# Local attention of a decoder kernel: one product per head on 64 rows, softmax over eight heads at once, and another order of the slots

## The chip, the cores and the metric

The kernel runs on one core of one Trainium2 chip. A core has engines that run side by side and meet at semaphores: PE (TensorE, matrix products), DVE (VectorE), ACT (ScalarE), POOL (GpSimd) and SP (SyncE, which starts transfers). The metric is the device time of one execution in microseconds (us), the median of the runs.

## What is computed

The reference is a decoder of two blocks on 32 sequences of 128 tokens with 128 features: a bidirectional state-space layer, cross attention and a mixture of experts with two experts a token, then local attention, cross attention and a mixture with one expert a token. The part that matters here is the local attention, cut from the reference to its mathematics, for one sequence `x` (128 x 128):

```
h      = layernorm(x)
q      = rmsnorm(h @ wq.T)  as 16 heads of 64      k, v = h @ wk.T, h @ wv.T  as 4 heads of 64, k with rmsnorm
score  = q_head @ k_(head//4).T / 8, allowed where i >= j and i - j < 64
x      = x + concat_heads(softmax(score) @ v_(head//4)) @ wo.T
```

## The kernel before

`window_attention_layer` (from L1743) computes this for 32 sequences, all of whose `x` stays in SBUF. T is 128 tokens, HL 16 heads, KVL 4 key/value heads, HDL 64 features a head, QH 4 heads a "quad", NQ 4 quads a sequence, NP 8 pairs of heads.

The work is a software pipeline. `walk_sequences` calls, on every engine, `slot(b, q)` for b = sequence and q = 0 to 3; `b.plus(k)` is the sequence k later, which is skipped where it isn't real. Within a slot an engine does its pieces in the order in which they stand in the text, each for its own sequence. Each piece waits for semaphores and raises one; `due(...)` drops waits for counts that aren't positive. The last argument of `walk_sequences` says how many sequences ahead the earliest piece works: it sets how many iterations are written out ahead of and behind the hardware loop.

The steps of one sequence, with the lines of the profile:

- SP loads the two experts' outputs into `back` (L1798); POOL adds them into `both` (L2076); DVE adds that to x (L1981), takes statistics (L2021, L2023, L2025); POOL makes the reciprocal root `xr` by a power (L2082); DVE normalises into `xh` (L2018).
- PE turns `xh` (L1859), ACT evicts it to `xT` (L1932), PE projects q into `pq` and k, v into `pkv` (L1867, L1869).
- ACT squares q and k (L1950, L1953) and copies v (L1958). DVE sums the squares (L2031) and makes `mean_sq` (L2035). POOL raises it to the power -0.5 in one instruction on 20 values a token (L2099, `r`). DVE multiplies q and k with it (L2042, L2045), writing each k head twice.
- PE turns qn and kn (L1878, L1881); ACT evicts `qT` (L1938, two) and `kT` (L1943, two halves of 64 partitions). `kT` holds k twice per head: in the upper 64 rows for one head of a pair, in the lower 64 rows for the other, with zeros elsewhere, which are written once ahead of the loop (L1968).
- Per quad, `scores`: PE writes the mask into one of two PSUM tiles `ps` with an identity product (L1829) and adds two products of 128 rows and 256 columns, each for a pair of heads (L1831). DVE takes the maximum `top` (L1996) and subtracts it (L2009), ACT takes the exponential (L1919), DVE sums (`den`, L1990) and inverts (`rden`, L2003), POOL multiplies (L2089, semaphore `norm_ready`).
- `turn` (L1819) turns the four heads of a quad into `pt`; ACT evicts `prT` (L1925); `values` multiplies with v into `py` in two halves of 64 columns of the array (L1843); ACT evicts `cT` (L1913). The projection back is L1890, then DVE adds it to x (L2059) and takes statistics (L2062).

Which piece stands in which slot sets the order. Before, in slot q: PE turn(b, q), scores(b+1, q), then in slot 1 the turns of xh (b+3) and of q and k (b+2), in slot 2 the projections (b+3) and the projection back (b-1), and at the end values of the quad before. ACT: cT of two quads before, Exp, prT(b, q), then in slot 1 xT, qT and kT, in slot 2 the squares. POOL: slot 0 `both` (b+4) and a normalisation; slot 1 a normalisation; slot 2 `xr` (b+4) and a normalisation; slot 3 a normalisation and the power (b+3). DVE makes `mean_sq` (b+3) in slot 3.

Of the kernel before, what the change touches and what calls it, by code (L numbers as in the profile page):

```python
# [36 lines left out]
QH = 4  # L37
# [1705 lines left out]
def window_attention_layer(nc, S, W, routed, ahead):  # L1743
# [12 lines left out]
    with ExitStack() as ctx:  # L1756
# [17 lines left out]
        kT = [A.sb(f"kT{p}", [128, KVL, 2, T]) for p in range(2)]  # L1774
        top, den, rden = ([A.sb(f"{n}{q}", [128, QH]) for q in range(NQ)] for n in ("top", "den", "rden"))
        pr = [A.sb(f"pr{q}", [128, QH, T]) for q in range(NQ)]
        prT = [A.sb(f"prT{q}", [128, QH, T]) for q in range(2)]
        cT = [A.sb(f"cT{p}", [128, NP, T]) for p in range(2)]
        ps = [A.ps(f"ps{k}", [128, QH, T]) for k in range(2)]
# [7 lines left out]
            exp_ready den_ready rden_ready norm_ready pt_mm prT_ready y_mm cT_ready o_mm x_ready stats kT_zero""".split()}  # L1787
        routed_in = [A.sem(f"routed_in{p}") for p in range(2)]
        rows_of = routed.rearrange("(k r) d -> r k d", k=K0)
        with nc.Block() as block:  # L1790
# [16 lines left out]
            def _(pe):  # L1807
# [4 lines left out]
                def turn(b, q):  # L1812

                    t = b.quad(q)
                    pe.wait_ge(s["norm_ready"], t + 1)
                    if due(t):
                        pe.wait_ge(s["prT_ready"], t)
                    for i in range(QH):
                        ins = tr(pt[:, i, :], pr[q][:, i, :], S.ident[:, :])  # L1819
                    ins.then_inc(s["pt_mm"], 1)  # L1820

                def scores(b, q):
                    t = b.quad(q)
                    if q == 0:
                        pe.wait_ge(s["qT_ready"], 2 * (b.n + 1))
                        pe.wait_ge(s["kT_ready"], 2 * (b.n + 1))
                    if due(t - 1):
                        pe.wait_ge(s["sub_ready"], t - 1)
                    mm(ps[q % 2][:, :, :], S.ident_bf[:, :], bc(outside[:, :], 1, QH), start=True, stop=False)  # L1829
                    for k in range(2):  # L1830
                        ins = mm(ps[q % 2][:, 2 * k:2 * k + 2, :], qT[b.p][:, 2 * q + k, :], kT[b.p][:, q, :, :],  # L1831
                                 start=False, stop=k == 1)
                    ins.then_inc(s["s_mm"], 1)

                def values(b, q):
# [6 lines left out]
                    for k in range(2):  # L1842
                        ins = mm(py[64 * k:64 * k + 64, 0:2 * T], v[b.p][:, q, :], prT[q % 2][:, k:QH:2, :],  # L1843
                                 start=True, stop=True)
                    ins.then_inc(s["y_mm"], 1)

                def slot(b, q):
                    if b.real():
                        turn(b, q)
                    nxt = b.plus(1)  # L1850
                    if nxt.real():
                        scores(nxt, q)
                    n = b.plus(3)
                    o = b.plus(-1)
# [5 lines left out]
                    if q == 2 and n.real():  # L1860
                        pe.wait_ge(s["xT_ready"], n.n + 1)
                        if due(2 * n.n):
                            pe.wait_ge(s["qT_ready"], 2 * n.n)
                        if due(2 * n.n):
                            pe.wait_ge(s["kT_ready"], 2 * n.n)
                        for k in range(2):
                            mm(pq[k][:, :], xT[:, :], W.wq[:, 512 * k:512 * k + 512], start=True, stop=True  # L1867
                               ).then_inc(s["qkv_mm"], 1)
                        mm(pkv[:, :], xT[:, :], W.wkv[:, :], start=True, stop=True).then_inc(s["qkv_mm"], 1)  # L1869
                    m = b.plus(2)  # L1870
                    if q == 1 and m.real():
                        pe.wait_ge(s["qn_ready"], 2 * (m.n + 1))
                        pe.wait_ge(s["kn_ready"], m.n + 1)
                        pe.wait_ge(s["ve_ready"], m.n + 1)
                        for k in range(2):
                            for i in range(4):
                                pair = 4 * k + i
                                ins = tr(pq[k][:, i * T:(i + 1) * T], qn[:, 2 * pair:2 * pair + 2, :], S.ident[:, :])  # L1878
                            ins.then_inc(s["qkT_mm"], 1)
                        for i in range(KVL):  # L1880
                            ins = tr(pkv[:, i * T:(i + 1) * T], kn[:, i, :, :], S.ident[:, :])  # L1881
                        ins.then_inc(s["qkT_mm"], 1)
                    if q == 2 and o.real():
# [8 lines left out]
                    last = b if q else b.plus(-1)  # L1892
                    if last.real():
                        values(last, (q - 1) % NQ)

                walk_sequences(pe, slot, 4)

            @block.scalar
            def _(act):
                A_ = nc.scalar.activation  # L1900
                act.wait_ge(s["kscale"], 2)
                act.wait_ge(s["kT_zero"], 2)

                def slot(b, q):

                    y = b if q >= 2 else b.plus(-1)
                    if y.real():
# [8 lines left out]
                    if e.real():  # L1916
                        qe = (q + 2) % NQ
                        act.wait_ge(s["sub_ready"], e.quad(qe) + 1)
                        A_(pr[qe][:, :, :], pr[qe][:, :, :], ACT.Exp).then_inc(s["exp_ready"], 1)  # L1919
# [6 lines left out]
                    n = b.plus(3)  # L1926
                    m = b.plus(2)
# [5 lines left out]
                    if q == 1 and m.real():  # L1933
                        if due(NQ * (m.n - 1)):
                            act.wait_ge(s["s_mm"], NQ * (m.n - 1))
# [5 lines left out]
                        for k in range(2):  # L1941
# [3 lines left out]
                    if q == 2 and n.real():  # L1945
# [9 lines left out]
                    if q == 3 and n.real():  # L1955
# [5 lines left out]
                walk_sequences(act, slot, 4)  # L1961

            @block.vector
            def _(dve):
                V = nc.vector
                dve.wait_ge(W.loaded, W.all())
                for p in range(2):
                    V.memset(kT[p][:, :, :, :], 0.0).then_inc(s["kT_zero"], 1)  # L1968
# [6 lines left out]
                def slot(b, q):  # L1975
                    d = b if q < 3 else b.plus(1)
                    w = b.plus(4)
                    if q == 1 and w.real():
                        i = bass.ds(w.n, 1)
                        dve.wait_ge(s["both_ready"], w.n + 1)  # L1980
                        V.tensor_tensor(S.x[:, i, :], S.x[:, i, :], both[w.p][:, :, :], ALU.add  # L1981
                                        ).then_inc(s["in_ready"], 1)
                        dve.wait_ge(s["in_ready"], w.n + 1)
                    if q == 2 and w.real():
                        dve.wait_ge(s["xbn_ready"], w.n + 1)
                    if d.real():
                        qd = (q + 1) % NQ
                        t = d.quad(qd)
                        dve.wait_ge(s["exp_ready"], t + 1)
                        V.tensor_reduce(den[qd][:, :], pr[qd][:, :, :], AX.X, ALU.add).then_inc(s["den_ready"], 1)  # L1990
# [645 lines left out]
```

## Time and profile before

| what | value |
|---|---|
| median of 3 runs | 2474.86 us (2468.1 to 2481.22) |
| the profiled execution | 2475.35 us, its span 2473.6 us |
| PE busy over the span | 2084.3 us (84%) |
| DVE, ACT, POOL busy | 1880.5, 1434.6, 1430.9 us (76, 58, 58%) |
| local attention | about 1514 to 2045 us of the span |

The span is the time between the first and the last instruction of the profiled execution. The stage that is changed is about a fifth of it; the other stages are the same in both kernels. "Busy" is the share of time in which an engine has an instruction in work; matrix products are pipelined, so PE's share is a little generous. In the rows below, a line of a timeline gives the start, the duration, the engine and the line of the kernel, the operation, what it writes and reads, and how many are merged; in square brackets stands how long the engine stood idle ahead of it and on whom it waited. A float product is recorded as two instructions.

### The profile page before, as it was taken

The numbers are of one execution on the slowest core, as the hardware profiler recorded it, in microseconds if no ns is written. First come the engines' busy times: TensorE is split into PE (matmuls) and PEld (weight loads), VectorE is DVE, ScalarE is ACT, GpSimd is POOL, SyncE is SP. The second block draws the span as 40 slices with busy tenths as digits, with TensorE's granted clock in tenths as the row PEclk, the third lists the DMA queues.
The fourth block names the chain that finished last, engine by engine and source line by source line (L and its number), as shares of the span: only waits on it lengthen the run. The fifth ranks groups of instructions, "written<-read, shape, count | busy, mean of one in ns | idle before, by whom it ended". The sixth has DMA issues, their size and how long they took to land. (4 is left out here: it accounts for less than half of the span.)

```text
span 2473.6 us, 43829 instructions
## 1 busy us (share of the span) xinstructions
PE 2084.3 (84%) x13248; PEld 1325.8 (54%) x13248; DVE 1880.5 (76%) x3129; ACT 1434.6 (58%) x2678; POOL 1430.9 (58%) x1094
## 2 busy tenths in 40 slices
PE   3888888888888886899874884899999998998486
PEld 1333343333333333677643773566666666776476
DVE  5999999999999997577653333788888885777445
ACT  4667676666666663466542452566666664665254
POOL 4788878777878886333244453455555542332546
PEclk7999999999999999799977997899999997999588
DMA  4222222222222221200111220000000001000442
GB/s 121 74 75 71 78 74 73 73 74 69 75 70 73 75 75 47 74 11 11 31 38 53 83 82 24 9 9 8 8 8 8 6 1 57 12 12 13 139 144 72
DMA packets 104420, 130.66 MB, mean 53 GB/s; under 512 B 33668, under 2 KB 65718, under 8 KB 103632
## 3 DMA queue, kind: packets, MB, share of 16 engines
q1 hardware_dynamic: 95600, 111.19, 15.4%
q0 software_dynamic: 8192, 17.59, 2.0%
q8 instruction: 48, 0.79, 0.1%
q10 hardware_dynamic: 512, 0.53, 0.1%
q14 instruction: 68, 0.56, 0.1%
HBM read 111.16 MB, written 25.20 MB: 55 GB/s over the span
## 5 line engine op out<-in xcount | busy, mean ns | idle before, releaser
L829 POOL TENSOR_TENSOR m_hc<-m_h,m_cs 128x1024 f32<-128x1024 f32 x256 | 602.8, 2359 | 183.2 <-DVE m_h L739 167.6
L739 DVE TENSOR_TENSOR_SCAN m_h<-m_da,m_pdb 128x1024 f32<-128x1024 f32 x256 | 585.2, 2286 | 27.7 <-DVE m_pdb L711 3.9
L432 PE MATMUL m_py<-m_hc,ident 128*128 128x512 f32 x1024 | 505.6, 618 | 1.9 <-POOL m_hc L829 1.9
L614 ACT ACTIVATE m_da<-m_dt,m_aneg 128x508 f32<-128x508 f32 x512 | 331.8, 709 | 117.2 <-DVE m_h L739 102.5
L711 DVE TENSOR_TENSOR m_pdb<-m_du,m_pdb 128x1024 f32<-128x1024 f32 x256 | 309.1, 1208 | 26.2 <-PE m_pdb L419 17.0
L432 PEld LDWEIGHTS m_py<-m_hc,ident 128*128 128x128 f32 x1024 | 199.4, 197 | 222.5 <-issue 211.8
L1082 ACT ACTIVATE x_prT<-x_pt 77x512 f32<-77x512 f32 x256 | 138.1, 586 | 135.5 <-PE x_pt L984 134.8
L1198 POOL TENSOR_TENSOR x_kd<-x_kT,x_hm 128x308 f32<-128x308 f32 x64 | 45.1, 705 | 278.7 <-ACT x_v_raw L1094 278.7
L419 PE MATMUL m_pdb<-m_bcrow,m_sel 96*128 96x512 bf16 x256 | 101.0, 396 | 111.1 <-DVE m_h L739 111.0
L2089 POOL TENSOR_TENSOR d_pr<-d_pr,d_rden 128x512 f32<-128x512 f32 x128 | 132.3, 1037 | 92.7 <-DVE d_rden L2003 92.5
L2099 POOL TENSOR_TENSOR d_r<-d_mean_sq,minus_half 128x20 f32<-128x20 f32 x32 | 113.4, 3542 | 76.1 <-DVE d_mean_sq L2035 76.1
L419 PEld LDWEIGHTS m_pdb<-m_bcrow,m_sel 96*128 96x128 bf16 x256 | 25.6, 100 | 228.0 <-DVE m_h L739 182.8
L984 PE MATMUL x_pt<-ident,x_pr 128*77 128x128 f32 x1024 | 142.0, 283 | 0.2
L984 PEld LDWEIGHTS x_pt<-ident,x_pr 128*77 128x77 f32 x1024 | 120.0, 152 | 28.3 <-issue 24.0
L1831 PE MATMUL d_ps<-d_kT,d_qT 128*128 128x256 f32 x512 | 134.1, 385 | 0.0
L378 PE MATMUL m_pm<-m_xnT,m_wtap 128*128 128x512 f32 x256 | 125.4, 614 | 1.3 <-ACT m_xnT L529 1.3
L1144 DVE TENSOR_REDUCE x_top<-x_ps 128x8 f32<-128x616 f32 x128 | 101.9, 796 | 31.3 <-PE x_ps L1003 12.4
L1728 POOL DMA_INDIRECT c_routed<-c_done,c_to x80 | 78.6, 983 | 74.6 <-DVE c_done L1699 49.7
L1150 DVE TENSOR_TENSOR x_pr<-x_ps,x_top 128x616 f32<-128x616 f32 x128 | 102.3, 800 | 15.9 <-DVE x_top L1144 3.5
L1130 DVE RECIPROCAL x_rden<-x_pyo 128x128 f32<-128x128 f32 x64 | 61.3, 958 | 68.9 <-PE x_pyo L1038 68.9
L1913 ACT ACTIVATE d_cT<-d_py 128x256 f32<-128x256 f32 x128 | 49.1, 384 | 108.6 <-PE d_py L1843 107.8
L999 PE MATMUL x_ps<-x_kd,x_qT 32*128 32x308 f32 x512 | 106.9, 495 | 4.3 <-issue 3.3
(309 smaller groups left out, 4647.8 us busy)
## 6 DMA issues: line engine op xcount, KB each, us to landing
m_cs<-crow SPq DMA_DIRECT2D x256, 256.0 KB, 3.1
f_row<-f_sorted SPq DMA_DIRECT2D x24, 400.0 KB
c_row<-c_sorted SPq DMA_DIRECT2D x40, 144.0 KB
d_back<-c_routed SPq DMA_DIRECT2D x32, 128.0 KB
f_sorted<-in_F_blank SPq DMA_DIRECT2D x9, 400.0 KB
cw_gud<-in_C_gud SPq DMA_DIRECT2D x1, 3456.0 KB
x<-in_x SPq DMA_DIRECT2D x8, 256.0 KB, 4.8
fw_w<-in_F_w SPq DMA_DIRECT2D x1, 2048.0 KB, 8.6
```

The costliest lines, as they stand in the source:

```text
L378: ins = mm(pm[1 - c][:, :], wtap[:, d, k, c * 128:(c + 1) * 128], xnT[:, par[0], :, off:off + T], start=k == 0, stop=k == TAPS - 1)
L419: mm(pdb[:, row_bank(n), :], sel[:, n, :], bcrow[d][:, :], start=True, stop=True).then_inc(s["b_mm"], 1)
L432: ins = mm(py[:, c, :], S.ident[:, :], hc[n % BUF][:, c, :], start=False, stop=n == NS - 1)
L614: A_(dst, src, ACT.Exp, scale=aneg[:, d, c, n:n + 1]).then_inc(s["da_ready"], 1)
L711: V.tensor_tensor(out, du[d][:, ::-1, :], bc(pdb[:, row_bank(n), :], 1, CH), ALU.mult).then_inc(s["db_ready"], 1)
L739: V.tensor_tensor_scan(h[n % BUF][:, way], da[n % BUF][:, d:d + CH * GT][:, way], pdb[:, b:b + 2, :].rearrange("p c t -> p (c t)")[:, way] ...
L829: P.tensor_tensor(hc[n % BUF][:, :, :], h[n % BUF][:, :].rearrange("p (c t) -> p c t", c=CH), bc(cs[n % BUF][:, :], 1, CH), ALU.mult).then ...
L984: ins = tr(pt[e][0:TC, i * T:(i + 1) * T], pr[u.p][u.h][:, QH * e + i, :], S.ident[:, :])
L1082: A_(prT[u.p][Q2 * u.h + e][:, :], pt[e][0:TC, :], ACT.Copy).then_inc(s["prT_ready"], 1)
L1831: ins = mm(ps[q % 2][:, 2 * k:2 * k + 2, :], qT[b.p][:, 2 * q + k, :], kT[b.p][:, q, :, :], start=False, stop=k == 1)
L2089: P.tensor_tensor(pr[qd][:, :, :], pr[qd][:, :, :], bc(rden[qd][:, :], 2, T), ALU.mult).then_inc(s["norm_ready"], 1)
L2099: P.tensor_tensor(r[:, :], mean_sq[:, :], S.minus_half[:, 0:NH], ALU.pow).then_inc(s["r_ready"], 1)
```

## The change

- **Scores.** `kT` is [128, KVL, T], without zeros: each k head stands in both halves of the partitions, and one eviction writes it. A head's product takes 64 rows of the array (`half`) and 128 columns; eight heads (a "pair" of quads, `pair(b, e)`, e = 0, 1) are made at once into one PSUM tile `ps` of two banks, the heads of the upper half in one bank and those of the lower in the other, ahead of them two mask products. `scores` stands in slots 0 and 2.
- **Softmax.** `top`, subtract, Exp, `den` and `rden` work on eight heads. POOL still normalises four heads at a time, two instructions in each of slots 1 and 3. `top`/subtract and `den`/`rden` stand in slots 1 and 3 of DVE, Exp in slots 0 and 2 of ACT.
- **Slots.** PE: the projections (b+3) move from slot 2 to slot 3, the turns of q and k from slot 1 to slot 2, the projection back from slot 2 to slot 1, and `values` ahead of these. ACT: qT and kT in slot 2, the squares and the copy of v in slot 3. DVE: the sum of squares and `mean_sq` in slot 0, for b+2; qn and kn in slot 2. POOL: the power in slot 0, alone; the normalisations in slots 1 and 3; `xr` and `both` (b+5) in slot 2.
- The heads are stored in another order, which `values` and the rows of `wo` follow. The walk runs five sequences ahead instead of four.

The core of the diff:

```diff
-        kT = [A.sb(f"kT{p}", [128, KVL, 2, T]) for p in range(2)]
-        top, den, rden = ([A.sb(f"{n}{q}", [128, QH]) for q in range(NQ)] for n in ("top", "den", "rden"))
-        pr = [A.sb(f"pr{q}", [128, QH, T]) for q in range(NQ)]
+        kT = [A.sb(f"kT{p}", [128, KVL, T]) for p in range(2)]
+        top, den, rden = ([A.sb(f"{n}{k}", [128, 2 * QH]) for k in range(4)] for n in ("top", "den", "rden"))
+        pr = [A.sb(f"pr{k}", [128, 2 * QH, T]) for k in range(4)]
-        ps = [A.ps(f"ps{k}", [128, QH, T]) for k in range(2)]
+        ps = A.ps("ps", [128, 2 * QH, T])
...
-                    if due(t - 1):
-                        pe.wait_ge(s["sub_ready"], t - 1)
-                    mm(ps[q % 2][:, :, :], S.ident_bf[:, :], bc(outside[:, :], 1, QH), start=True, stop=False)
-                    for k in range(2):
-                        ins = mm(ps[q % 2][:, 2 * k:2 * k + 2, :], qT[b.p][:, 2 * q + k, :], kT[b.p][:, q, :, :],
-                                 start=False, stop=k == 1)
+                    if due(pair(b, e)):
+                        pe.wait_ge(s["sub_ready"], pair(b, e))
+                    for h in range(2):
+                        mm(ps[:, of(h), :], S.ident_bf[:, :], bc(outside[:, :], 1, QH), start=True, stop=False)
+                    for i in range(QH):
+                        kv = 2 * e + i // 2
+                        for h in range(2):
+                            half = slice(64 * h, 64 * h + 64)
+                            ins = mm(ps[:, QH * h + i, :], qT[b.p][half, 2 * kv + i % 2, :], kT[b.p][half, kv, :],
+                                     start=False, stop=i == QH - 1)
                     ins.then_inc(s["s_mm"], 1)
...
+                    if nxt.real() and q % 2 == 0:
+                        scores(nxt, q // 2)
...
+                    last = b if q else o
+                    if last.real():
+                        values(last, (q - 1) % NQ)
+                    if q == 1 and o.real():
                         pe.wait_ge(s["cT_ready"], NQ * (o.n + 1))
...
+                    if q == 2 and m.real():
+                        pe.wait_ge(s["qn_ready"], 2 * (m.n + 1))
...
+                    if q == 3 and n.real():
+                        pe.wait_ge(s["xT_ready"], n.n + 1)
...
-                        for k in range(2):
-                            half = slice(64 * k, 64 * k + 64)
-                            A_(kT[m.p][half, :, k, :], pkv[half, :].rearrange("p (i t) -> p i t", t=T), ACT.Copy,
-                               scale=kscale[half, 0:1]).then_inc(s["kT_ready"], 1)
+                        A_(kT[m.p][:, :, :], pkv[:, :].rearrange("p (i t) -> p i t", t=T), ACT.Copy,
+                           scale=kscale[:, 0:1]).then_inc(s["kT_ready"], 1)
...
-                for p in range(2):
-                    V.memset(kT[p][:, :, :, :], 0.0).then_inc(s["kT_zero"], 1)
...
+                    if q % 2 and d.real():
+                        dve.wait_ge(s["exp_ready"], pair(d, ed) + 1)
+                        V.tensor_reduce(den[kd][:, :], pr[kd][:, :, :], AX.X, ALU.add).then_inc(s["den_ready"], 1)
...
+                    if q == 0 and g.real():
+                        dve.wait_ge(s["sq_ready"], 3 * (g.n + 1))
...
+                    d, ed = (b, 1) if q < 3 else (b.plus(1), 0)
+                    kd = 2 * d.p + ed
+                    g, w, v = b.plus(2), b.plus(4), b.plus(5)
+                    if q % 2 and d.real():
+                        pool.wait_ge(s["rden_ready"], pair(d, ed) + 1)
+                        for h in range(2):
+                            P.tensor_tensor(pr[kd][:, of(h), :], pr[kd][:, of(h), :], bc(rden[kd][:, of(h)], 2, T),
+                                            ALU.mult).then_inc(s["norm_ready"], 1)
+                    if q == 0 and g.real():
+                        pool.wait_ge(s["ms_ready"], g.n + 1)
...
```

## Rows read from the trace of the kernel before

**Rows 1.** Windows, 1600-2000: us, busy (instructions) of each engine, PEclk, DMA share, GB/s.
```profile
1600.00:2000.00 400.00, 386.68 (x2272) 269.57 (x2271) 351.75 (x757) 266.06 (x547) 223.88 (x182) 1.00 0.03 8
```

**Rows 2.** Waits, 1600 to 2000: us in total, times, longest.
```profile
PEld d_pt L1819 <- POOL d_pr L2089: 35.1, 52, 1.0
```

**Rows 3.** Timeline of one period: start us, us, engine line, what, wait.
```profile
1808.66 3.54 POOL L2099 TENSOR_TENSOR d_r<-d_mean_sq,minus_half 128x20 f32<-128x20 f32 x1 [2.04 <-DVE d_mean_sq L2035]
...
1812.16 0.45 POOL L2076 TENSOR_TENSOR d_both<-d_back 128x128 f32<-128x128 f32 x1
...
1812.57 1.04 POOL L2089 TENSOR_TENSOR d_pr<-d_pr,d_rden 128x512 f32<-128x512 f32 x1
...
1813.67 0.66 PE L1819 MATMUL d_pt<-ident,d_pr 128*128 128x128 f32 x4 [0.52 <-POOL d_pr L2089]
...
1814.16 0.38 PE L1829 MATMUL d_ps<-d_outside,ident_bf 128*128 128x512 bf16 x1
...
1814.38 1.03 PE L1831 MATMUL d_ps<-d_kT,d_qT 128*128 128x256 f32 x4
...
1815.24 0.27 PE L1859 MATMUL d_px<-ident,d_xh 128*128 128x128 f32 x1
...
1815.35 1.04 PE L1878 MATMUL d_pq<-ident,d_qn 128*128 128x128 f32 x8
...
1815.99 1.08 ACT L1938 ACTIVATE d_qT<-d_pq 128x512 f32<-128x512 f32 x2
...
1816.75 0.65 PE L1843 MATMUL d_py<-d_prT,d_v 128*64 128x256 f32 x4
...
1816.96 1.38 ACT L1943 ACTIVATE d_kT<-d_pkv,d_kscale 64x512 f32<-64x512 f32 x2
...
1817.34 0.66 PE L1819 MATMUL d_pt<-ident,d_pr 128*128 128x128 f32 x4
...
1818.36 0.38 ACT L1913 ACTIVATE d_cT<-d_py 128x256 f32<-128x256 f32 x1
...
1818.91 1.88 PE L1867 MATMUL d_pq<-dw_wq,d_xT 128*128 128x512 f32 x4
...
1823.62 0.18 DVE L2035 TENSOR_SCALAR d_mean_sq<-d_ssq 128x20 f32<-128x20 f32 x1
...
1824.03 3.54 POOL L2099 TENSOR_TENSOR d_r<-d_mean_sq,minus_half 128x20 f32<-128x20 f32 x1 [2.07 <-DVE d_mean_sq L2035]
```

**Rows 4.** Timeline, PE in cross attention, 2165.8 to 2166.9.
```profile
2165.86 0.27 PE L1022 MATMUL x_pqkv<-ident,x_xh 128*128 128x128 f32 x1
2166.07 0.79 PE L999 MATMUL x_ps<-x_kd,x_qT 32*128 32x308 f32 x4
2166.79 0.31 PE L1003 MATMUL x_ps<-x_out_of,x_fill 128*128 128x308 bf16 x1
```

**Rows 5.** Groups of lines and one line (min/median/max ns): 512 and 616 elements.
```profile
L1990 DVE TENSOR_REDUCE d_den<-d_pr 128x4 f32<-128x512 f32 x105 | 71.9, 685 | 15.0 <-ACT d_pr L1919 12.0
...
L1919 ACT ACTIVATE d_pr<-d_pr 128x512 f32<-128x512 f32 x104 | 64.9, 624 | 0.6
...
L1144 DVE TENSOR_REDUCE x_top<-x_ps 128x8 f32<-128x616 f32 x128 | 101.9, 796 | 31.3 <-PE x_ps L1003 12.4
...
L1076 ACT ACTIVATE x_pr<-x_pr x128: 710/717/719, 1003.4 to 2274.8; 128x616 f32<-128x616 f32 x128
```

**Rows 6.** The power of all sequences (first, last start), and the last statistics.
```profile
L2099 POOL TENSOR_TENSOR d_r<-d_mean_sq,minus_half x32: 3538/3541/3575, 1527.4 to 2007.9; 128x20 f32<-128x20 f32 x32
...
2044.57 0.29 DVE L2062 BATCH_NORM_STATS2 bn<-x 128x6 f32<-128x128 f32 x1
```

**Rows 7.** PE after two long waits, and windows with PEclk beside them.
```profile
1581.64 0.33 PE L1819 MATMUL d_pt<-ident,d_pr 128*128 128x128 f32 x1 [2.16 <-POOL d_pr L2089]
...
1582.30:1585.70 3.40, 3.40 (x14) 2.82 (x13) 3.35 (x7) 0.88 (x3) 1.04 (x1) 0.53 0.05 14
...
1443.30 0.38 PE L1442 MATMUL c_pd<-c_wt,c_h 128*128 128x128 f32 x1 [1.89 <-DVE c_h L1689]
...
1440.00:1450.00 10.00, 8.11 (x51) 7.08 (x49) 3.62 (x11) 4.62 (x10) 5.60 (x6) 1.00 0.29 79
```

More of the change, by code:

```diff
@@ L1849, in slot @@
                         turn(b, q)
[L1850 to L1854, printed above, removed]
+                    nxt, m, n, o = (b.plus(k) for k in (1, 2, 3, -1))
+                    if nxt.real() and q % 2 == 0:
+                        scores(nxt, q // 2)
                     if q == 1 and n.real():
@@ L1915, in slot @@
                     e = b if q < 2 else b.plus(1)
[L1916 to L1919, printed above, removed]
+                    if e.real() and q % 2 == 0:
+                        half = (q + 2) % NQ // 2
+                        p = pr[2 * e.p + half]
+                        act.wait_ge(s["sub_ready"], pair(e, half) + 1)
+                        A_(p[:, :, :], p[:, :, :], ACT.Exp).then_inc(s["exp_ready"], 1)
                     if b.real():
@@ L1975, in slot @@
                 def slot(b, q):
-                    d = b if q < 3 else b.plus(1)
-                    w = b.plus(4)
+                    d, a = (b, b.plus(1)) if q < 3 else (b.plus(1), b.plus(1))
+                    ed, ea = (1, 0) if q < 3 else (0, 1)
+                    kd, ka = 2 * d.p + ed, 2 * a.p + ea
+                    c, g, m, n, w, o = (b.plus(k) for k in (1, 2, 2, 3, 4, -1))
                     if q == 1 and w.real():
[L1979 to L1982, printed above, removed]
@@ L1984, in slot @@
                     if q == 2 and w.real():
                         dve.wait_ge(s["xbn_ready"], w.n + 1)
[L1986 to L1990, printed above, removed]
-                    a = b if q < 1 else b.plus(1)
-                    if a.real():
-                        qa = (q + 3) % NQ
-                        t = a.quad(qa)
-                        dve.wait_ge(s["s_mm"], t + 1)
-                        V.tensor_reduce(top[qa][:, :], ps[qa % 2][:, :, :], AX.X, ALU.max
-                                        ).then_inc(s["top_ready"], 1)
@@ L2037, in slot @@
-                    if q == 0 and m.real():
+                    if q == 2 and m.real():
                         dve.wait_ge(s["r_ready"], m.n + 1)
@@ L2048, in slot @@
                                         ).then_inc(s["kn_ready"], 1)
-                    c = b.plus(1)
+                    if q == 2 and w.real():
+                        V.bn_aggr(xmv[w.p][:, :], xbn[w.p][:, :]).then_inc(s["xmv_ready"], 1)
+                        dve.wait_ge(s["xmv_ready"], w.n + 1)
+                        V.tensor_scalar(xve[w.p][:, :], xmv[w.p][:, 1:2], LN_EPS, None, ALU.add
+                                        ).then_inc(s["xve_ready"], 1)
                     if q == 2 and c.real():
@@ L2070, in slot @@
                 def slot(b, q):
[L2071 to L2077 removed]
+                    d, ed = (b, 1) if q < 3 else (b.plus(1), 0)
[8 more added lines that the diff above has]
+                        pool.wait_ge(s["ms_ready"], g.n + 1)
+                        if due(2 * g.n):
+                            pool.wait_ge(s["qn_ready"], 2 * g.n)
+                        if due(g.n):
+                            pool.wait_ge(s["kn_ready"], g.n)
+                        P.tensor_tensor(r[:, :], mean_sq[:, :], S.minus_half[:, 0:NH], ALU.pow
+                                        ).then_inc(s["r_ready"], 1)
                     if q == 2 and w.real():
```

192 lines of the change are left out of this document (80 added, 112 removed).

## The prediction

> **What bounds the kernel now.** I read the windows view first: between 1600 and 2000 us, where the loop of local attention runs undisturbed, PE is busy 387 of 400 us, DVE 352, ACT 266, POOL 224, at full clock [rows 1]. That looks like a PE bound. The view of waits, read next, speaks against it: PE's weight load stood 35 us, 52 times, twice a sequence, for POOL's normalisation [rows 2]. So I read the timeline of one period [rows 3] and followed it back from that wait. `mean_sq` (L2035) starts at 1808.25, one period before the row at 1823.62; POOL's power (L2099) starts 0.41 us later and takes 3.54; `both` (L2076) and one normalisation (1812.57, 1.04) follow; the turn at 1813.67 waits for that. Then PE works in its order to the projections at 1818.91, ACT squares them, DVE sums them, and the next `mean_sq` starts at 1823.62. The sum, 5.42 (1808.25 to 1813.67) + 5.24 (to 1818.91) + 4.71 (to 1823.62) = 15.37 us, is exactly the distance between the powers at 1808.66 and 1824.03. This ring through POOL, PE, ACT and DVE sets the period; no engine's sum does. What counts of the change is what it puts into the ring.
>
> **The new ring.** In the new order `mean_sq` of sequence b+2 is made in slot (b, 0), POOL's power follows there, then the normalisations of b's second half in slot 1, which turn(b, 2) waits for; PE goes on with scores(b+1, 1), values(b, 1), the twelve turns of q and k of b+2, turn(b, 3), values(b, 2), the projections of b+3; their squares give the next `mean_sq`. Again one period long. Its terms, from [rows 3] unless said otherwise:
>
> (1) POOL. From `mean_sq` to power 0.41, power to next instruction 3.50 (1808.66 to 1812.16), normalisation to turn 1.10 (1812.57 to 1813.67): 5.01. `both`, 0.41 (1812.16 to 1812.57), is out of the ring; xr and `both` now stand behind the normalisations. Before it was 5.42.
>
> (2) Turn to scores: 0.49 (1813.67 to 1814.16), as before.
>
> (3) Scores of eight heads. A mask product of 512 columns takes 0.22 (1814.16 to 1814.38); two take 0.43. Before, two products of 256 columns took 0.86 (1814.38 to 1815.24, where the turn of xh stood, L1859, whose 0.11 falls to the next row). Per column that is four times the mask's 0.22 / 512 (it is float, the mask bf16), so 128 columns cost 0.213 and eight of them 1.71 one after another. On two 64-row halves of the array they can run in pairs. No row has 64-row products; the nearest is cross attention, with two 32-row products of 308 columns: from their start to the next line 0.72 us [rows 4], where two in sequence would take 4 passes of 0.128, twice, 1.03 alone. In parallel they are 0.51, which leaves 0.21: about 0.11 for weights that could not be loaded ahead and 0.10 until the full array starts. In front of them 2165.86 to 2166.07 is 0.21 for a turn of 0.11, so another 0.10. I take in parallel: 0.43 + 0.10 + 0.11 + 0.86 + 0.10 = 1.59. Bounds: 1.29 with no switching, 2.45 in sequence.
>
> (4) values: 0.59 (1816.75 to 1817.34), unchanged; its two operands are other slices of the same size.
>
> (5) From the first turn of q and k (S) to the projections. PE alone would need 1.3 for twelve turns (1815.35 to 1816.75, less 0.1), turn 0.49, values 0.59: 2.4. But values(b, 2) waits for cT(b, 1), since `py` is one buffer, and ACT has cT(b, 1) in slot 3, behind the evictions of q and k in slot 2. qT starts 0.64 after the turns (1815.35 to 1815.99), two take 0.97 until kT (1816.96), kT one instruction instead of two 0.70 (1816.96 to 1818.36 for two), cT 0.38: S + 2.70. Add 0.15 to wake PE and 0.59: projections at S + 3.4. The ring pays 1.0 more than PE's work. Bounds 2.4 and 3.7.
>
> (6) Projections to `mean_sq` 4.71, unchanged.
>
> Period: 5.01 + 0.49 + 1.59 + 0.59 + 3.42 + 4.71 = 15.81 us, against 15.37: +0.44.
>
> **What is hidden.** DVE: den and top of 8 heads in one instruction. 512 elements take 0.685 us, 616 take 0.796 [rows 5], so 1024 about 1.23; three such kinds save 0.14 each, twice, with two reciprocals some 1.2 us a sequence. DVE's work falls to about 12.4 us of 15.8. I laid its order out: from `mean_sq` (0) add at 0.1, den at 0.3, top at 1.9, sub 3.2 to 4.4, qn 4.4, kn to 6.3, den of the next half 7.8, top 9.2, sub to 11.7, xh; then it waits for the squares at 14.3. Not late anywhere, and nothing gained. Exp of eight heads: 0.62 for 512, 0.72 for 616 [rows 5], so 1.10; the one at 4.5 ends at 5.6, just before turn(b, 2) has been made (5.7). That slack is thin, but qT stands 2 us behind it. kT in one eviction saves 0.70, which is in (5). The single `ps` makes scores wait for the last sub: it ends at 4.4 and the scores want it at 5.5; the other at 11.7, they want it at 14.1. PE itself has about 13.3 us of work and stands 1.3 us before turn(b, 2). Two memsets at the start run beside the first `back` transfer: nothing. The new weight order costs nothing.
>
> A rule of the Trainium skill bears on (3): TensorEngine Tiling (Array Packing), Key Properties, says that changing the tiling mode drains the engine. The 0.10 on either side of the products in [rows 4] agrees. By a count of array passes alone, without such drains, the period would be 15.50 and the whole 2475 + 29 × 0.13.
>
> **Ends of the stage.** There are 32 powers, from 1527.4 to 2007.9 [rows 6], 31 intervals. In the first two nothing but the ring through kT acts, and one kT eviction fewer gives 0.7 each: -1.4. The other 29: 29 × 0.44 = +12.8. From the last power to the last statistics (2007.9 to 2044.6, end 2044.9) it is 37.0 us for 12 turns, 3.1 each; the last power now stands one turn later in the order: -3.1. Sum +8.3.
>
> The profiled run took 2475.35 us (span 2473.6), 0.5 over the median of 2474.86. 2475.35 + 8.3 = 2483.7; beside the median 2483.2. I forecast 2483, with 2473 to 2494 for this case: its period can be off by 0.3 us, which is 9 us. A difference below 0.5%, 12.4 us, is about what a measurement of this kernel can't tell from none.
>
> **Rivals.** (B) The halves don't run in pairs: the eight products take 1.71, the period 16.67, the total 2475.35 - 4.5 + 29 × 1.30 = 2508.5. For it: no row shows 64 rows of 128-column float products, where weights (0.11) are as long as the product. Against it: [rows 4], and values, whose two 64-column halves, 4 x 0.213 in sequence, take 0.59 with everything. Chance 0.10.
>
> A sentence of the same page, that tiles load weights and multiply independently, would give the forecast and not B; [rows 4] agrees for 32 rows only.
>
> (C) PE's longer wait (1.3 us, plus 0.9 in slot 3) lets its clock fall each period. After a wait of 2.16 us in the first sequences the clock was 0.53 for the next 3.4 us; in the experts' stage a wait of 1.89 left it at 1.00 [rows 7]. Half of such a stretch would be lost in the ring, 1.7 us a period: 2475.35 + 8.3 + 49 = 2533. [...] Chance 0.05.
>
> (D) Faster: the ring's (5) is PE's own 2.4, because cT(b, 1) or kT come earlier than I have them, and the switching in (3) is absent: 15.81 - 1.0 - 0.3 = 14.5, total 2475.35 - 4.5 - 25 = 2446; with the first alone 14.8 and 2454. For it: ACT has only 9 us of work a sequence. Against it: the order of ACT's instructions. Chance 0.11.
>
> (E) The halves are parallel but a second wait joins the ring: DVE's dependent pairs (den then reciprocal, top then sub) are no longer interleaved. If they delayed qn and the turns of q and k by more than 1.8 us, the ring would go through them; at +0.3 a period, 2492. Chance 0.08.
>
> **How the numbers follow.** Forecast 0.66, B 0.10, C 0.05, D 0.11, E 0.08. Slower by over 0.5% (2487.2 of the median): B, C, most of E, and 0.2 of the forecast's 0.66: 0.35. Faster (below 2462.5): D, 0.11. Within: 0.54. The range 2458 to 2508 takes in the forecast, E, part of B and the edge of D, and leaves out some 2 in 10.
>
> **What would show it.** Powers 15.8 us apart in the loop; turn(b, 2) waiting for POOL about 1.3 us; from mask to values 1.6 us for eight heads (2.4 under B); 3.4 us from the turns of q to the projections (2.4 under D), with ACT's cT last before the values; PE's clock 1.00; DVE busy about 315 of 400 us. The forecast is wrong if the wait of turn(b, 2) isn't for the power's successor, or if the projections wait for something else.

## The result and the profile after

The changed kernel takes 2480.4 us (median of 20 runs) against 2470.3 for the kernel before (20 runs). The measured ratio is 1.0033, 95% interval 1.0022 to 1.0044; the two medians alone would make 1.0041. So the change makes the kernel slower by a third of a per cent, a small difference but clear of the noise. The forecast's +8.3 us is 1.0034. The profiled execution took 2484.49 us, its span is 2482.6.

The windows view of the same stretch as [rows 1] (us, busy time and instructions of PE, PEld, DVE, ACT and POOL, PEclk, DMA share, GB/s), kernel after:

```profile
1600.00:2000.00 400.00, 350.94 (x2592) 230.68 (x2592) 318.21 (x531) 228.95 (x452) 216.56 (x178) 1.00 0.03 8
```

PE is busy 36 us less than in [rows 1], DVE 34 us less, ACT 37 us less, and the kernel is not faster. By busy time every engine has room. The ring, the chain of steps that leads from one sequence's `mean_sq` to the next one's, has not.

The timeline of one period, kernel after, answers to [rows 3] (start us, us, engine line, what, wait):

```profile
1818.76 0.18 DVE L2048 TENSOR_SCALAR d_mean_sq<-d_ssq 128x20 f32<-128x20 f32 x1
...
1819.16 3.55 POOL L2077 TENSOR_TENSOR d_r<-d_mean_sq,minus_half 128x20 f32<-128x20 f32 x1 [5.27 <-DVE d_mean_sq L2048]
...
1822.68 2.04 POOL L2069 TENSOR_TENSOR d_pr<-d_pr,d_rden 128x512 f32<-128x512 f32 x2
...
1823.78 0.66 PE L1828 MATMUL d_pt<-ident,d_pr 128*128 128x128 f32 x4 [0.79 <-POOL d_pr L2069]
...
1824.27 0.59 PE L1838 MATMUL d_ps<-d_outside,ident_bf 128*128 128x512 bf16 x2
...
1824.79 1.16 PE L1843 MATMUL d_ps<-d_kT,d_qT 64*128 64x128 f32 x16
...
1825.88 0.65 PE L1855 MATMUL d_py<-d_prT,d_v 128*64 128x256 f32 x4
...
1826.47 1.09 PE L1888 MATMUL d_pq<-ident,d_qn 128*128 128x128 f32 x8
...
1827.16 1.09 ACT L1946 ACTIVATE d_qT<-d_pq 128x512 f32<-128x512 f32 x2 [1.96 <-PE d_pq L1888]
...
1828.13 0.69 ACT L1949 ACTIVATE d_kT<-d_pkv,d_kscale 128x512 f32<-128x512 f32 x1
...
1828.70 0.40 ACT L1922 ACTIVATE d_cT<-d_py 128x256 f32<-128x256 f32 x1
...
1829.24 0.65 PE L1855 MATMUL d_py<-d_prT,d_v 128*64 128x256 f32 x4 [0.81 <-ACT d_cT L1922]
...
1829.82 1.98 PE L1901 MATMUL d_pq<-dw_wq,d_xT 128*128 128x512 f32 x4
...
1834.64 0.18 DVE L2048 TENSOR_SCALAR d_mean_sq<-d_ssq 128x20 f32<-128x20 f32 x1
```

Read it as the chain from `mean_sq` to `mean_sq`. The two waits in brackets on PE are where the ring comes to PE from another engine: from POOL at the first turn, and from ACT's `cT` at the second values. From the turns of q to that second values the ring runs through ACT (`qT`, `kT`, `cT`), and behind the projections through ACT's squares and DVE's sum, which are not shown. The line of the 64-row products has 16 parts: eight products of two array passes each. From their start to the next line it is 1.09 us (1824.79 to 1825.88).

Two rows of the waits view, 1600 to 2000, kernel after (us in total, times, longest), in the place of [rows 2]:

```profile
PE d_pt L1828 <- POOL d_pr L2069: 21.0, 26, 0.9
PE d_py L1855 <- ACT d_cT L1922: 20.9, 25, 0.9
```

Each comes once a period with some 0.8 us: the power's wait at turn(b, 2), and the wait for `cT` ahead of values(b, 2), which the kernel before did not have.

The power of all sequences, and the last statistics (answer to [rows 6]):

```profile
L2077 POOL TENSOR_TENSOR d_r<-d_mean_sq,minus_half x32: 3537/3549/3554, 1531.2 to 2025.4; 128x20 f32<-128x20 f32 x32
...
2058.06 0.29 DVE L2032 BATCH_NORM_STATS2 bn<-x 128x6 f32<-128x128 f32 x1
```

From the first to the last power it is 494.2 us, before 480.5.

### The profile page after: what moved, and what is told of

The parts are those of the page before. It is cut to its first block and busy times, and to the rows that moved or that the text cites. A ratio compares the mean times of both kernels' runs of the same rounds, so it can differ in the third digit from the quotient of the medians.

```text
span 2482.6 us, 44194 instructions
## 1 busy us (share of the span) xinstructions
PE 2057.6 (83%) x13760; PEld 1290.2 (52%) x13760; DVE 1849.0 (74%) x2871; ACT 1399.7 (56%) x2582; POOL 1429.4 (58%) x1094
## 5 line engine op out<-in xcount | busy, mean ns | idle before, releaser
L2044 DVE TENSOR_REDUCE d_ssq<-d_sq 128x20 f32<-128x1280 f32 x32 | 47.5, 1486 | 94.1 <-ACT d_sq L1959 94.1
L1150 DVE TENSOR_TENSOR x_pr<-x_ps,x_top 128x616 f32<-128x616 f32 x128 | 102.4, 800 | 14.1
L1929 ACT ACTIVATE d_pr<-d_pr 128x1024 f32<-128x1024 f32 x64 | 67.8, 1059 | 72.3 <-DVE d_pr L2000 72.3
```

## The experiments

e1 to e4 ran on one chip (kernel before 2472.33 us, 17 runs), e5 to e7 on another (kernel before 2413.44, 14 runs), and the row of the kernel after is the result above; on the second chip what is ahead of this stage was some 50 us shorter in every kernel. So ratios are taken within a chip only, and the traces are compared by the distance of successive powers in the loop, which the clock of 1.00 makes comparable. That distance, from the timeline rows of POOL's power between 1620 and 1900 us (it alternates between two values, as the loop holds two sequences; their mean is given):

| kernel | powers apart, us | ratio to before, 95% interval |
|---|---|---|
| before | 15.37 | 1 |
| after | 15.91 (15.88, 15.93) | 1.0033 [1.0022, 1.0044] |
| e1_ct_early | 15.03 (15.00, 15.05) | 0.9908 [0.9889, 0.9928] |
| e2_grouped | 16.46 (16.43, 16.49) | 1.0102 [1.0076, 1.0129] |
| e3_fours | 15.91 (15.88, 15.94) | 1.0022 [1.0008, 1.0036] |
| e4_padded | 17.38 (17.35, 17.40) | 1.0184 [1.0160, 1.0208] |
| e5_both_late | 15.06 (15.01, 15.11) | 0.9962 [0.9947, 0.9976] |
| e6_project_early | 14.28 | 0.9837 [0.9820, 0.9854] |
| e7_half_power | 15.22 (15.14, 15.31) | 0.9924 [0.9902, 0.9946] |

**e1_ct_early: is the wait for `cT` in the ring?** The kernel after, with ACT's `cT` of (b, 1) ahead of the evictions of q and k.

```diff
-                    y = b if q >= 2 else b.plus(-1)
...
-                    if y.real():
-                        qy = (q - 2) % NQ
...
+                    def evict(y, qy):
+                        if y.real():
...
+                    if q != 3:
+                        evict(b if q == 2 else b.plus(-1), (q - 2) % NQ)
...
+                    if q == 2:
+                        evict(b, 1)
```

(`evict` holds the old body of the `cT` piece. The last two lines stand between ACT's `prT` and its `qT`; (b, 1) had its turn in slot 3.)

> The changed kernel, with ACT's eviction cT(b, 1) moved from the head of slot 3 to slot 2, ahead of the evictions of q and k. Theory (the ring mean_sq, power, normalisation, turn(b, 2), scores, values, turns of q and k, values(b, 2), projections, squares sets the period): in the changed kernel's trace values(b, 2) waits 0.87 us for cT(b, 1), which stands behind qT, qT, kT. ACT is idle 2.1 us before qT, so the move costs nothing. From the turns of q to the projections 3.35 becomes about 2.45, the period 15.88 becomes 15.0, 31 periods give -28 us: ratio to the kernel before about 0.992. Rival (the sum of an engine's work sets the period, PE at 88% with its fixed gaps): no work is taken away, so no change, ratio 1.003.

The timeline of e1_ct_early, from the turns of q to the projections:

```profile
1816.93 1.09 PE L1888 MATMUL d_pq<-ident,d_qn 128*128 128x128 f32 x8
...
1817.05 0.38 ACT L1922 ACTIVATE d_cT<-d_py 128x256 f32<-128x256 f32 x1 [1.52 <-PE d_py L1855]
...
1818.65 0.69 ACT L1954 ACTIVATE d_kT<-d_pkv,d_kscale 128x512 f32<-128x512 f32 x1
...
1818.83 0.65 PE L1855 MATMUL d_py<-d_prT,d_v 128*64 128x256 f32 x4
...
1819.49 1.10 PE L1901 MATMUL d_pq<-dw_wq,d_xT 128*128 128x512 f32 x2
```

`cT` now runs while the turns of q do, the values row has no bracket, and the way to the projections is 2.56 us in place of 3.35. The period fell by 0.88, of which this is 0.79. One ACT instruction of 0.38 us in another place turns the change from 0.3% slower into 0.9% faster: the wait for `cT` was in the ring.

**e2_grouped: do the halves pair, and does the order of issue matter?** The same eight products, four on the upper rows and then four on the lower.

```diff
-                    for i in range(QH):
-                        kv = 2 * e + i // 2
-                        for h in range(2):
+                    for h in range(2):
+                        for i in range(QH):
+                            kv = 2 * e + i // 2
...
```

> The changed kernel, with the eight 64-row products of a scores block issued four on the upper half and then four on the lower half, instead of alternating. Theory: the halves run in parallel only with a partner next in the queue; grouped, only the seam overlaps. The products take 1.6 us instead of 0.86, from mask to values 2.4 instead of 1.61, the ring +0.75 a period: +23 us, ratio about 1.013. It also prices my rival B of the prediction (no pairing at all: +0.85 a period). Rival: the queue looks far enough ahead to pair them in any order: no change, ratio 1.003.

Timeline of PE, e2_grouped:

```profile
1808.80 0.59 PE L1838 MATMUL d_ps<-d_outside,ident_bf 128*128 128x512 bf16 x2
1809.32 1.71 PE L1843 MATMUL d_ps<-d_kT,d_qT 64*128 64x128 f32 x16
1810.96 0.65 PE L1855 MATMUL d_py<-d_prT,d_v 128*64 128x256 f32 x4
```

From the products to values it is 1.64 us against 1.09, +0.55, and the period grew by 0.55 (15.91 to 16.46). So the pairs are real where the halves alternate, and mostly lost where they don't. In sequence the block would have cost the 0.86 of the pairs once more, and I had expected +0.75 (a ratio of 1.013 where 1.0102 came out); +0.55 says that more overlap is left than the seam alone. Which products still overlap stays open. Each half writes a PSUM bank of its own here, so e2 groups the banks together with the halves, and no run tells the two apart.

**e3_fours: what do the merged instructions of eight heads bring?** The kernel after, with den, top, subtraction and Exp again as two instructions of four heads.

```diff
-                        V.tensor_reduce(den[kd][:, :], pr[kd][:, :, :], AX.X, ALU.add).then_inc(s["den_ready"], 1)
+                        V.tensor_reduce(den[kd][:, of(0)], pr[kd][:, of(0), :], AX.X, ALU.add)
+                        V.tensor_reduce(den[kd][:, of(1)], pr[kd][:, of(1), :], AX.X, ALU.add).then_inc(s["den_ready"], 1)
...
```

> The changed kernel, with den, top, subtraction and Exp again as two instructions of four heads each, in the same places. DVE gets about 0.9 us more work a sequence, ACT 0.35. Theory: DVE waits 2.3 us a period for the squares and none of these steps is in the ring, so nothing changes: ratio 1.003, within 0.002. Rival (DVE's chain of dependent steps is what holds qn and the turns of q and k): the subtraction ends 0.3 us later and qn with it, so up to +0.3 a period, +9 us, ratio 1.007; with DVE as the bound +28 us, 1.014.

Rows of e3_fours: two of den in the timeline, and the window.

```profile
1804.26 0.67 DVE L1988 TENSOR_REDUCE d_den<-d_pr 128x4 f32<-128x512 f32 x1
1804.85 0.68 DVE L1989 TENSOR_REDUCE d_den<-d_pr 128x4 f32<-128x512 f32 x1
...
1600.00:2000.00 400.00, 351.36 (x2583) 230.65 (x2584) 326.62 (x679) 231.85 (x503) 215.71 (x176) 1.00 0.03 7
```

The period is that of after to 0.01 us. The second den starts 0.59 after the first, before the first's 0.67 are over; both take 1.27 from start to end, where one of eight heads takes 1.20 to 1.22. DVE is busy 8.4 us more in 400, 0.33 a period. So merging is worth little on DVE's own account, and nothing in the total.

**e4_padded: what do the 64-row products and the single `kT` eviction bring?** The kernel after, with `kT` padded with zeros again, four products of 128 rows and 256 columns for eight heads, and two evictions of `kT`; slots as in after.

```diff
-                    for i in range(QH):
-                        kv = 2 * e + i // 2
-                        for h in range(2):
-                            half = slice(64 * h, 64 * h + 64)
-                            ins = mm(ps[:, QH * h + i, :], qT[b.p][half, 2 * kv + i % 2, :], kT[b.p][half, kv, :],
-                                     start=False, stop=i == QH - 1)
+                    for h in range(2):
+                        kv = 2 * e + h
+                        for k in range(2):
+                            ins = mm(ps[:, QH * h + 2 * k:QH * h + 2 * k + 2, :], qT[b.p][:, 2 * kv + k, :],
+                                     kT[b.p][:, kv, :, :], start=False, stop=k == 1)
...
```

> The changed kernel with its 64-row products undone: kT holds zeros again and is evicted in two parts, the scores of eight heads are two masks and four products of 128 rows and 256 columns; slots, softmax over eight heads and everything else as in the changed kernel. Theory: from mask to values 1.61 becomes 0.43 + 1.71 + 0.10 = 2.24, and a second kT eviction adds 0.70 between the turns of k and values(b, 2): the ring 15.88 + 1.33 = 17.2, +41 us, ratio about 1.020. Rival (PE's sum counts, ACT's eviction is hidden): only the PE part, +0.63 a period, +20 us, ratio 1.011.

Timeline of e4_padded, mask to projections:

```profile
1807.01 0.59 PE L1838 MATMUL d_ps<-d_outside,ident_bf 128*128 128x512 bf16 x2
...
1809.26 0.65 PE L1854 MATMUL d_py<-d_prT,d_v 128*64 128x256 f32 x4
1809.84 1.09 PE L1887 MATMUL d_pq<-ident,d_qn 128*128 128x128 f32 x8
...
1811.51 1.38 ACT L1951 ACTIVATE d_kT<-d_pkv,d_kscale 64x512 f32<-64x512 f32 x2
...
1813.44 0.65 PE L1854 MATMUL d_py<-d_prT,d_v 128*64 128x256 f32 x4 [1.63 <-ACT d_cT L1922]
1814.03 0.70 PE L1900 MATMUL d_pq<-dw_wq,d_xT 128*128 128x512 f32 x1
```

Mask to values is 2.25 against 1.61 (+0.64), turns of q to projections 4.19 against 3.35 (+0.84), where the second half of the eviction delays `cT` and `cT` the values, which wait 1.63 for it. Together 1.48; the period grew by 1.47. I had expected 1.33: from the start of `kT` to that of `cT` it is 1.40 us (1811.51 to 1812.91) against 0.57 in the kernel after (1828.13 to 1828.70), 0.83 more and not 0.70. So this part of the change is worth 1.5 us a period, and the rest of the change costs more than that: 17.38 - 15.37 = 2.01. The rest is the new order of the slots and the softmax over eight heads; e3 leaves the period as it is with the merged instructions undone, so the 2.01 lies in the order. How it divides among the moved pieces is shown for `cT` alone (e1).

**e5_both_late: is `both` in the ring of the kernel before?** Only `both` is moved, from between the power and the normalisation to behind it.

```diff
@@ POOL, slot 0, kernel before
-                    if q == 0 and w.real():
-                        ...
-                        P.tensor_tensor(both[w.p][:, :, :], back[w.p][:, 0:1, :], back[w.p][:, 1:2, :], ALU.add
-                                        ).then_inc(s["both_ready"], 1)
...
+                    if q == 0 and w.real():
+                        ...
+                        P.tensor_tensor(both[w.p][:, :, :], back[w.p][:, 0:1, :], back[w.p][:, 1:2, :], ALU.add
+                                        ).then_inc(s["both_ready"], 1)
```

> The kernel before, with one thing of the change alone: POOL adds `both` in slot 0 behind the normalisation instead of ahead of it. Nothing else is touched. Theory: `both` stands between the power and the normalisation that turn(b, 1) waits for, so it is in the ring of the kernel before; without it the period is 15.37 - 0.41 = 14.96, as PE has 1.0 us of waiting to give. 31 periods: -12.7 us, ratio 0.995. Rival (PE's own work, 97% busy, sets the period): no change, ratio 1.000.

Timeline of POOL, e5_both_late, and further on the wait for the next normalisation:

```profile
1778.85 3.54 POOL L2099 TENSOR_TENSOR d_r<-d_mean_sq,minus_half 128x20 f32<-128x20 f32 x1 [1.75 <-DVE d_mean_sq L2035]
1782.35 1.04 POOL L2083 TENSOR_TENSOR d_pr<-d_pr,d_rden 128x512 f32<-128x512 f32 x1
1783.35 0.45 POOL L2089 TENSOR_TENSOR d_both<-d_back 128x128 f32<-128x128 f32 x1
...
1786.17 1.04 POOL L2083 TENSOR_TENSOR d_pr<-d_pr,d_rden 128x512 f32<-128x512 f32 x1 [2.37 <-DVE d_rden L2003]
...
1786.53 0.65 PE L1843 MATMUL d_py<-d_prT,d_v 128*64 128x256 f32 x4
...
1787.26 0.42 PEld L1819 LDWEIGHTS d_pt<-ident,d_pr 128*128 128x128 f32 x4 [0.54 <-POOL d_pr L2083]
```

The normalisation follows the power by 3.50 and `both` is out. The period fell by 0.31 where the ring alone gives 0.41 (in half of the periods it is 15.01, 0.36 less; in the other half 15.11). The ring of the kernel before is confirmed by an edit that takes no work away. The other 0.10 goes to a second wait, which the last three lines show: the next turn now waits for POOL's next normalisation, which had itself waited for DVE's `rden`. From values to that turn it is 0.74 us (0.64 in the other half of the periods), where [rows 3] had 0.59 (1816.75 to 1817.34).

**e7_half_power: is the power in the ring, and what stands behind it?** The kernel after with the power on 10 of the 20 columns; the other half of the root's values is left out.

```diff
-                        P.tensor_tensor(r[:, :], mean_sq[:, :], S.minus_half[:, 0:NH], ALU.pow
+                        P.tensor_tensor(r[:, 0:10], mean_sq[:, 0:10], S.minus_half[:, 0:10], ALU.pow
...
```

> The changed kernel with POOL's power on 10 of the 20 columns; the other ten of r stay 1 (written once), so that ten heads are not normalised: this is work left out. Theory: the power is in the ring with its whole time. Ten columns should take about 2.0 us instead of 3.54 (the one-column power takes 0.57). The ring falls by 1.55, but PE's wait before turn(b, 2) is only 1.0 (0.85 to 1.3), and behind that PE's own order sets turn(b, 2): the period falls by about 1.1, -34 us, ratio 0.989. Rival (POOL is 54% busy and off the path): no change, ratio 1.003.

Timeline of e7_half_power, from `mean_sq` to the projections and the next `mean_sq`:

```profile
1782.39 0.18 DVE L2048 TENSOR_SCALAR d_mean_sq<-d_ssq 128x20 f32<-128x20 f32 x1
...
1782.79 1.97 POOL L2079 TENSOR_TENSOR d_r<-d_mean_sq,minus_half 128x10 f32<-128x10 f32 x1 [4.48 <-DVE d_mean_sq L2048]
...
1786.03 1.22 DVE L2000 TENSOR_TENSOR d_pr<-d_ps,d_top 128x1024 f32<-128x1024 f32 x1
...
1786.45 0.60 PE L1828 MATMUL d_pt<-ident,d_pr 128*128 128x128 f32 x4
...
1787.32 0.61 PE L1838 MATMUL d_ps<-d_outside,ident_bf 128*128 128x512 bf16 x2 [0.26 <-DVE d_pr L2000]
...
1788.94 0.65 PE L1855 MATMUL d_py<-d_prT,d_v 128*64 128x256 f32 x4
...
1792.88 1.98 PE L1901 MATMUL d_pq<-dw_wq,d_xT 128*128 128x512 f32 x4
...
1797.70 0.18 DVE L2048 TENSOR_SCALAR d_mean_sq<-d_ssq 128x20 f32<-128x20 f32 x1
```

The power is 1.58 us shorter, the period only 0.69, and I had expected 1.1: a miss. The turn no longer waits for POOL, but the masks now wait for DVE's subtraction, which frees the single `ps`. A second ring takes over: `mean_sq`, then den, top and the subtraction in DVE's order, masks (4.93 from 1782.39 to 1787.32), then as before (1.62 + 3.94 + 4.82): 15.31 us, this period's length. In the kernel after, `mean_sq` to masks is 5.51 through POOL. So in this half of the periods the ring through POOL is only 0.58 longer than the one through DVE (15.88 against 15.31). In the other half `mean_sq` to masks is 4.70 (1797.70 to 1802.40, where the subtraction had ended at 1802.35) against 5.50 in the kernel after (1834.64 to 1840.14), and the period fell from 15.93 to 15.14. On the mean the slack is 0.69, and that is all that a faster power can give as long as the rest stays.

**e6_project_early: a version built on these readings.** The kernel after with both its waits taken out of the ring by order alone, no work changed. On PE, slot 2 goes turn(b, 2), turns of q and k (b+2), scores(b+1, 1), projections (b+3), and then values(b, 1); ACT's squares stand at the end of slot 2. The projections no longer stand behind values(b, 2), which waits for `cT`.

```diff
@@ PE, the turns of q and k: now ahead of scores, each half of q awaited by itself
-                        pe.wait_ge(s["qn_ready"], 2 * (m.n + 1))
...
+                            pe.wait_ge(s["qn_ready"], 2 * m.n + k + 1)
...
@@ PE, the projections: now between scores and values
-                    if q == 3 and n.real():
+                    if q == 2 and n.real():
...
@@ ACT, the squares
-                    if q == 3 and n.real():
+                    if q == 2 and n.real():
```

> The changed kernel with another order on PE in slot 2: turn(b, 2), the turns of q and k (each half of q as soon as DVE has it), scores(b+1, 1), the projections of b+3, then values(b, 1); slot 3 keeps turn(b, 3) and values(b, 2). ACT makes the squares and the copy of v at the end of slot 2. The same work, no instruction less. Theory: turns(q, k) no longer wait for scores and values, the evictions of q and k run beside scores, and values(b, 1), turn(b, 3), values(b, 2) leave the ring. The ring falls to 5.0 + 0.5 + 1.6 (turns) + 1.6 (scores) + 4.7 = 13.4, below PE's own work; PE then sets the period, about 14.1 to 14.3. 31 x -1.65: -51 us, ratio to the kernel before 0.983. Rival (the change is bound by PE's sum as it stands): ratio 1.003. If later values and evictions make a new chain through ACT, in between.

PE's timeline and the window of e6_project_early:

```profile
1782.31 0.60 PE L1828 MATMUL d_pt<-ident,d_pr 128*128 128x128 f32 x4
1782.74 1.04 PE L1869 MATMUL d_pq<-ident,d_qn 128*128 128x128 f32 x8
1783.62 0.60 PE L1873 MATMUL d_pkv<-ident,d_kn 128*128 128x128 f32 x4
1784.06 0.59 PE L1838 MATMUL d_ps<-d_outside,ident_bf 128*128 128x512 bf16 x2
1784.58 1.16 PE L1843 MATMUL d_ps<-d_kT,d_qT 64*128 64x128 f32 x16
1785.67 1.98 PE L1884 MATMUL d_pq<-dw_wq,d_xT 128*128 128x512 f32 x4
...
1600.00:1900.00 300.00, 291.81 (x2166) 190.66 (x2164) 265.27 (x443) 195.15 (x378) 179.73 (x147) 1.00 0.03 8
```

No line of this stretch carries a wait (the only one in the period is 0.26 us for ACT's `xT`), and PE is busy 97% of the time. [rows 1] had 97% too, with a ring as the bound, so the share alone proves nothing; here the timeline shows it: PE never waits for POOL, and the powers are 14.27 to 14.29 apart. At 2369.8 us and a ratio of 0.9837 to the kernel before, 1.6% faster, it beats both kernels, and it is what was expected of it (14.1 to 14.3 us, 0.983).

## Why the prediction came out right, step by step

The terms of the new ring, from the timeline after:

| term | forecast | measured |
|---|---|---|
| (1) `mean_sq` to turn | 5.01 | 5.02 (1818.76 to 1823.78) |
| (2) turn to masks | 0.49 | 0.49 |
| (3) masks to values | 1.59 | 1.61 |
| (4) values | 0.59 | 0.59 |
| (5) turns of q to projections | 3.42 | 3.35 |
| (6) projections to `mean_sq` | 4.71 | 4.82 |
| period | 15.81 | 15.88, in every second period 15.93 |

**The old ring.** That its terms add up to 15.37 proves nothing: distances from start to start along any chain from `mean_sq` to the next `mean_sq` make one period, and the 1808.25 was the 1823.62 less that period (the trace has the row at 1808.26). What carries the reading is that each link is tight, a wait for the step before it or work in an engine's order without a gap, and that e5 took `both` out of it and the period fell.

**Terms (1), (2), (4)** were rows taken over and held. That `both` leaves the ring was right; e5 shows it alone in the kernel before.

**Term (3)**, the only one without a row of its own, held in both its parts: the masks with the change of mode 0.52 (1824.27 to 1824.79; forecast 0.43 + 0.10), the 64-row block 1.09 (forecast 0.11 + 0.86 + 0.10). What [rows 4] showed for two 32-row products carried over to eight 64-row ones. The Trainium skill's drain at a change of mode (TensorEngine Tiling (Array Packing), Key Properties) agrees with these 0.1 us on either side. The prediction's count without such drains is off in two places: of the 0.3 that it takes out, 0.11 were for weights, and 2475 + 29 × 0.13 leaves out the -4.5 of the ends. The page's other sentence, that different tiles can load and multiply in parallel, says nothing of an order of issue. Read as holding for any order it would give e2 the same 1.09; e2 took 1.64, and the measurement decides: the halves pair when they alternate.

**Term (5)**: the chain that the prediction named, qT, kT, `cT`, values, is the one in the timeline, 0.07 shorter than forecast, with a wait of 0.81 on values. The 0.15 to wake PE, which had no row, is 0.14 (`cT` ends at 1829.10, values starts at 1829.24). e1 takes `cT` out of it and gets 2.56, near the 2.4 that PE alone was said to need.

**Term (6)** was called unchanged and was 0.11 longer. The four query projections take 1.98 (1.88 in [rows 3]). They now follow values, whose products use half of the columns, and their first weights are not loaded ahead: the first load of weights starts with the products at 1829.82, while in the kernel before it started at 1818.69, 0.22 ahead of them. It is the same 0.11 that the prediction had put on the scores' first weights, and was owed here too. With +0.02 in (3), +0.01 in (1) and -0.07 in (5) it makes up the 0.07 between 15.81 and 15.88.

**Hidden work.** Here the prediction mis-sized a term. It took three merged kinds at 0.14 saved each, twice, and two reciprocals: 1.2 us a sequence. DVE's busy time fell from 13.5 us a period (351.75 of 400 at 15.37) to 12.66 (318.21 at 15.91): 0.86. e3 says why: the 0.14 was 2 x 0.685 - 1.23, but successive instructions overlap, so two take 1.27 and not 1.37. It cost nothing in the total since DVE had room. But the room was thinner than the prediction's layout let it seem: the subtraction ended 4.9 us after `mean_sq`, not 4.4, and where the prediction gave the masks 1.1 us behind it (4.4 to 5.5), e7 puts the slack at 0.58 us, and at 0.80 in every second period. PE's wait for POOL was forecast at 1.3 and was 0.8; PE's own work is 13.95 us a period (350.94 of 400 at 15.91), not 13.3.

**The ends.** Forecast: the first two intervals -1.4, the drain -3.1, 29 periods of +0.44. Measured: from the first power to the fifth -0.9 (65.3 against 66.2 us), 23 periods of +0.54 (12.4), the last four intervals +2.2, together +13.7 where +11.4 was forecast; the drain from the last power to the end of the statistics 33.0 against 37.0 us, -4.0. That is +9.7 where +8.3 was forecast. The two spans differ by 9.0: the stages ahead, which are unchanged, ran 3.4 us longer in this execution, the way to the first power was 0.4 longer, and what stands behind ran 4.5 shorter. So the ring and the size of its terms were understood, but that 1.0033 meets 1.0034 is partly luck. The interval alone reaches 2.7 us to either side, the 31 periods cost 2.3 us more than forecast and the drain 0.9 less. The third interval after is 18.54 us; there PE waits for 3.26 us and its clock falls. Timeline of PE and window of that place, kernel after:

```profile
1566.62 1.11 PE L1828 MATMUL d_pt<-ident,d_pr 128*128 128x128 f32 x4 [3.26 <-POOL d_pr L2069]
...
1566.00:1570.00 4.00, 3.38 (x20) 2.49 (x22) 3.71 (x9) 1.65 (x2) 2.66 (x5) 0.50 0.00 0
```

The clock is at 1.2 GHz for these 4 us. So rival C's mechanism exists in the stage's first sequences, as [rows 7] had it in the kernel before, and does not reach the loop, where no wait of PE is longer than 0.9 us and the clock is 1.00.

**The rivals.** B (no pairs): refuted by term (3), and e2 shows what much of it would have looked like, +0.55 a period and 1.0102. D (term (5) is PE's own) was wrong for the kernel after, by the bracket on values, but e1 makes it true and lands at 0.9908; D with the first effect alone was 2454, 0.991 of 2475. What decided between the forecast and D was the place of one ACT instruction, as the prediction said. E (DVE delays qn and the turns of q) did not happen: qn ends at 1824.82 in the kernel after, 1.65 us ahead of the turns at 1826.47. The DVE chain that came near is another one, the subtraction that frees `ps` for the masks, with the 0.58 to 0.80 us of e7. That the net was a slowdown, with 36 us less busy time on PE, is settled by e4: the narrower products and the single eviction bring 1.5 us a period, the new order of the slots takes 2.0.

## What to carry to other kernels

Before costing an edit in a software pipeline, find the ring: start from the wait that ends last, go back from releaser to releaser until the same instruction of another sequence comes up, and check that every link is tight. The sum of the distances is the period whatever chain is taken, so it is no check; an edit that shortens one link and nothing else is (e1, e5). What an edit saves outside that ring is saved busy time and nothing else. One small instruction in the wrong place of an in-order engine can cost more than a whole family of halved products brings: here 0.38 us of `cT` cost 0.88 us a period (e1), and the halved products brought 0.64 (e4). Then ask for the second-longest ring, because it caps what shortening the first can give (0.69 us of 1.58 in e7).

## What the runs showed of the hardware that was not expected

- Products on the two 64-row halves of the array pair up only if they alternate in the order of issue: eight of 128 columns, float, took 1.09 us alternating and 1.64 grouped (each half with its own PSUM bank).
- Two DVE reductions in a row on 128x512 elements start 0.59 us apart though each lasts 0.67 to 0.68 (e3), so one of 1024 elements (1.20 to 1.22) saves some 0.05 us against two (1.27).
- POOL's power took 3.55 us on 128x20 values, 1.97 on 128x10 and 0.57 on 128x1: about 0.16 us a column, with some 0.4 fixed.
- A block of full-array products takes 0.1 us longer behind products on half of the columns (1.98 us for the four query projections against 1.88 behind full-array products), as its first weights are not loaded ahead. Behind products on half of the rows it takes 1.98 as well (e6).
